# Segment products of an edge block: head outermost instead of sub-block outermost

## What is computed

```python
h = jnp.einsum('nd,hdf->nhf', x, W)                      # 4 heads of 64
a_src = jnp.einsum('nhf,hf->nh', h, att_src)
a_dst = jnp.einsum('nhf,hf->nh', h, att_dst)
e = jax.nn.leaky_relu(a_src[src] + a_dst[dst], NEG_SLOPE)
emax = jax.ops.segment_max(e, dst, num_segments=N)
ex = jnp.exp(e - emax[dst])
denom = jax.ops.segment_sum(ex, dst, num_segments=N)
alpha = ex / denom[dst]
msg = h[src] * alpha[:, :, None]
out = jax.ops.segment_sum(msg, dst, num_segments=N)
```

## Time and profile before

| | us |
|---|---|
| median of 3 runs | 3192.11 |
| lowest and highest | 3185.83, 3193.67 |
| the profiled execution: its time | 3188.82 |
| the same: span from first to last instruction | 3187.0 |
| busy in it: TensorE matmuls / weight loads | 1814.2 / 1333.7 |
| VectorE / ScalarE / GpSimd | 1568.0 / 721.3 / 1911.1 |
| mean granted TensorE clock | 0.641 of full speed |
| first L1136 starts, last L1136 starts | 142.8, 2835.4 |

### The profile page before, as it was taken

One profiled execution on the slowest core, in us unless ns is written; L12 is line 12 of the kernel. 1 busy time (PEld: TensorE's weight loads), 2 busy tenths in 40 slices (PEclk: granted clock), 3 DMA queues, 4 the chain that ended last, 5 costly groups with the idle time before them and its releaser, 6 DMA issues. The chain is left out here.

```text
span 3187.0 us, 54639 instructions
## 1 busy us (share of the span) xinstructions
PE 1814.2 (57%) x17401; PEld 1333.7 (42%) x17401; DVE 1568.0 (49%) x5615; ACT 721.3 (23%) x2125; POOL 1911.1 (60%) x1849
## 2 busy tenths in 40 slices
PE   4666665556665445435435655665566566531995
PEld 3434443444444233223224533553354344321885
DVE  5566665556665454444444445453545444323332
ACT  3522221112222021012003222332232132211221
POOL 1366666666666666666676667666666766731343
PEclk9767765555555555555556666676576667655998
DMA  5244445534444533443355464455545644434787
GB/s 156 89 121 139 140 141 146 159 92 116 129 131 124 136 101 89 108 118 88 89 136 141 124 161 135 120 127 142 137 129 140 168 109 124 129 96 121 199 216 186
DMA packets 275873, 418.72 MB, mean 131 GB/s; under 512 B 70992, under 2 KB 206036, under 8 KB 275336
## 3 DMA queue, kind: packets, MB, share of 16 engines
q0 software_dynamic: 98592, 245.59, 30.3%
q1 hardware_dynamic: 173360, 167.20, 17.3%
q10 hardware_dynamic: 3640, 2.50, 0.3%
HBM read 341.18 MB, written 73.83 MB: 130 GB/s over the span
## 5 line engine op out<-in xcount | busy, mean ns | idle before, releaser
L911 POOL DMA_INDIRECT region<-node_table,region x1612 | 1615.6, 1002 | 979.0 <-issue 442.9
L1136 PE MATMUL ps_p<-region 128*32 128x65 f32 x12896 | 567.5, 290 | 917.4 <-issue 514.4
L1136 PEld LDWEIGHTS ps_p<-region 128*32 128x32 f32 x12896 | 377.8, 147 | 1114.4 <-issue 645.8
L1385 DVE SCALAR_TENSOR_TENSOR acc<-ps_p,region,acc 128x65 f32 x806 | 193.2, 281 | 611.8 <-remote 558.5
L1001 ACT ACTIVATE region<-ps_s 128x128 f32<-128x128 f32 x403 | 111.5, 277 | 1380.9 <-remote 991.4
L1377 DVE TENSOR_TENSOR region<-region 128x512 f32<-128x512 f32 x403 | 280.6, 696 | 147.2 <-DVE region L1361 51.3
L1118 PE MATMUL ps_s<-ident,region 128*128 128x128 f32 x403 | 164.5, 408 | 160.2 <-DVE region L1371 80.0
L1122 PEld LDWEIGHTS ps_s<-region 128*128 128x128 f32 x806 | 204.0, 281 | 94.9 <-issue 64.8
L1007 ACT ACTIVATE region<-region 128x16 f32<-128x16 f32 x403 | 86.9, 216 | 690.3 <-DVE region L1371 348.2
L1357 DVE TENSOR_SCALAR region<-drep,region 128x8 f32 x403 | 101.5, 252 | 258.2 <-issue 257.3
L1122 PE MATMUL ps_s<-region 128*128 128x32 f32 x806 | 191.8, 323 | 24.2 <-issue 23.3
(11 more groups left out here) (317 smaller groups left out, 2807.8 us busy)
## 6 DMA issues: line engine op xcount, KB each, us to landing
region<-in_W_dram SPq DMA_DIRECT2D x84, 512.0 KB
region<-node_table,region POOLq DMA_INDIRECT x1612
acc<-in_W_dram SPq DMA_DIRECT2D x28, 512.0 KB
acc<-base_rows SPq DMA_DIRECT2D x14, 896.0 KB, 5.3
qkv_rows<-region SPq DMA_DIRECT2D x49, 194.0 KB
region<-expert_in SPq DMA_DIRECT2D x28, 258.0 KB
xe<-expert_in SPq DMA_DIRECT2D x28, 258.0 KB, 4.0
node_table<-region SPq DMA_DIRECT2D x49, 132.0 KB, 1.7
```

What stands on the lines that cost most here:

```text
L911: pool.indirect_dma_start(out=rows[:, s, j, :], out_offset=None, in_=table[:, :], in_offset=bass.IndirectOffsetOnAxis(ap=idx[:, s * SUB + ...
L1136: m = pe.matmul(ps_p[s % 2][h * WIN:(h + 1) * WIN, 0:HC], wts[:, s % 2, j, h, :], rows[:, s, j, h * HC:(h + 1) * HC], start=j == 0, stop=j ...
L1385: m = dve.scalar_tensor_tensor(out=a, in0=ps_p[s % 2][:, 0:HC], scalar=here[:, k, at(n)], in1=a, op0=ALU.mult, op1=ALU.add)
```

## The change

The two loops around the matmul are swapped. All sixteen products, their operands, the `start` and `stop` flags and the increment on the last one stay. The last product is (j = 3, h = 3) in both orders.

```diff
@@ -1131,8 +1131,8 @@
                 pe.wait_ge(w_ready, n + 1)
                 if not isinstance(n, int) or n >= 2:
                     pe.wait_ge(block_done, n - 1)
-                for j in range(SUB):
-                    for h in range(G_HEADS):
+                for h in range(G_HEADS):
+                    for j in range(SUB):
                         m = pe.matmul(ps_p[s % 2][h * WIN:(h + 1) * WIN, 0:HC], wts[:, s % 2, j, h, :],
                                       rows[:, s, j, h * HC:(h + 1) * HC], start=j == 0, stop=j == SUB - 1)
                 m.then_inc(block_ps, 1)
```

## The result

| | before | after |
|---|---|---|
| median of 5 runs, us | 3185.83 | 3205.88 |
| lowest and highest | 3180.97, 3193.67 | 3199.32, 3211.06 |
| the profiled execution: time, span | 3188.82, 3187.0 | 3203.76, 3202.0 |
| mean granted TensorE clock | 0.641 | 0.703 |

The ratio of after to before is 1.0062, with a 95% interval of 1.0045 to 1.0079: the new order costs 0.6%, some 20 us. 3228 was forecast, so the sign was right and the size twice too large. Run again on two chips, each time beside the kernel before, the changed kernel came out at 1.0073 (1.0049 to 1.0096) and 1.0060 (1.0046 to 1.0073).

The account below looks back on a forecast made before the run. TensorE completions held while gathers move data were taken as the limit where that cycle runs. Carried blocks' 34 us and projection blocks' 5 us summed to +39 us on the profiled 3188.8, giving 3228 us; range 3100 to 3310.

Parts of the forecast that it names:

- The price of a burst (28 steps): TensorE's sixteen segment products: 28 steps between first and last start, adding 2.26 us at 1.2 GHz, 1.14 at 2.4.
- What of it reaches the end: Whole block loop: of 819 us added on TensorE, 39 us lengthen the run, the rest lies in idle time.
- Light blocks: zero: Blocks without extra TensorE work: ready anew after 4.2 us against a mean period of 6.7 us, so no cost.
- held blocks: hidden: Blocks whose TensorE completions are held during gathers: 12 released records take 1.6 instead of 0.66 us, at no cost.
- 5 stood: The 49 blocks with the projections: 0.1 us each, 5 us.
- the carried blocks' 34 us: Second-half blocks carrying an expert tile, TensorE nearly full: 0.3 us per block, 112 x 0.3 = 34 us.
- the first 244 blocks within 1%: Blocks before the carried expert tiles: the prediction is wrong if their time changes by over 1%.
- Weight loads hidden: Weight loads of the segment products on TensorE: still run beside the matmuls in the new order, adding nothing.
- Rival (d): Segment products: a group's weight load cannot run beside its matmul; about +1.5 us per block, 3790 us; chance 0.07.
- Rival (a), absorbed: Block loop: the holds of completions pace it and the added time sits inside them; 3182 to 3198 us; chance 0.18.
- Rival (b), shorter holds: Held completions in the loop: spreading the burst shortens the holds, -110 us, 3080 us; chance 0.18.
- Rival (c), the clock: TensorE in the loop: being busier, it is granted a higher clock, removing the carried term; 3165 to 3190 us; chance 0.07.

Follow-up runs that it names:

- blocks 0 to 243: The new order in blocks 0 to 243 only, the old order in the rest, against the kernel before: 1.0033 (1.0020 to 1.0046).
- blocks 244 to 402: The new order in blocks 244 to 402 only, the old order in the rest, against the kernel before: 1.0036 (1.0023 to 1.0048).
- blocks 0 to 151: The new order in blocks 0 to 151 only, the old order in the rest, against the kernel before: 1.0022 (1.0008 to 1.0035).
- blocks 152 to 243: The new order in blocks 152 to 243 only, the old order in the rest, against the kernel before: 1.0011 (0.9998 to 1.0024).
- two heads at a time: Kernel before, with the sub-blocks run through for heads 0 and 1 alternating, then 2 and 3: 1.0028 with holds, 0.9994 on the chip of 2825 us.
- three, then the fourth: Kernel before, with each head's sub-blocks 0 to 2 in a row, then the four products of sub-block 3: 1.0081 (1.0055 to 1.0108).
- 164 columns: Kernel before in its old order, each segment product streaming 164 columns instead of 65, VectorE still reading 65: 1.0091 (1.0072 to 1.0109).
- 236 columns: Kernel before in its old order, each segment product streaming 236 columns instead of 65, VectorE still reading 65: 1.0102 (1.0083 to 1.0120).
- the copy taken out: Gathers read row numbers from the resident table without waiting for ScalarE's copy; against the kernel before, old order 0.9978, new order 1.0031.
- the new order and 164 columns: Head order with 164 columns streamed per product instead of 65, against the kernel before on the chip of 2825 us: 1.0102 (1.0082 to 1.0122).

## Why the prediction was right in sign and twice too large

**The price of a burst (28 steps): the step that failed.** Forecast 3.35 and 1.80 us, measured 2.39 and 1.41: +1.30 us at 1.2 GHz and +0.75 at 2.4 instead of +2.26 and +1.14. "The next head's first can start beside the last of the one before" took for granted that records start in program order; the next head starts beside the fourth from the last. At the mean clocks of the earlier trace rows, 19 steps would add 1.23 us per block in the first half and 1.11 in the second, 477 us in all; the higher clock takes some of it back, and measured are 366.8, where the sum had put 819 us.

**What of it reaches the end.** The sum let 39 of 819 us through, 4.8%. Measured against the profiled busy time of L1136 (567.5 before):

| kernel | L1136 busy added, us | slower, us | share | wait for a slot grows by, us |
|---|---|---|---|---|
| the change | 366.8 | 19.7 | 5% | 33 |
| blocks 0 to 243 | 232.2 | 10.5 | 5% | 12 |
| blocks 244 to 402 | 116.8 | 11.5 | 10% | 39 |
| blocks 0 to 151 | 131.4 | 7.0 | 5% | 27 |
| blocks 152 to 243 | 98.4 | 3.5 | 4% | 4 |
| two heads at a time | 126.1 | 8.9 | 7% | 15 |
| three, then the fourth | 203.3 | 25.8 (17.5 to 34.4) | 13% | 34 |
| 164 columns | 429.3 | 29.0 | 7% | 39 |
| 236 columns | 642.4 | 32.5 | 5% | 61 |

All rows are from the chips of 3185 us. The last column is the sum of GpSimd's waits ahead of its gathers for L1136, "remote" and the copy of the row numbers, less the 427 us of before; each is of one profiled execution, and the two other profiles of the changed kernel give 24 and 31.

Four to seven hundredths in most rows, with "blocks 244 to 402" and "three, then the fourth" above them. The interval of the latter begins at 9%, so the share is no constant. For the change itself the share was about right and the price was not: 4.8% of 366.8 is 18 us. This is a regularity of these runs, not a cause.

**Where it lies: wrong.** "Light blocks: zero" and "held blocks: hidden" fail by 0.04 to 0.05 us per block in the first 244, 10.5 us where 5 stood; the carried blocks' 34 us were 11.5 for the whole last part. That the two errors cancel in the share above is luck. The bound that was set, the first 244 blocks within 1%, holds.

**What the light cost is.** The account that the runs fit best: the loop's pace is GpSimd's cycle of gathers, pause and gathers; the pause ends when products of an earlier block are done; and a longer burst moves that by a small part of its length. The waits ahead of L911 grew by 33 us with the change, and with the copy taken out, when the products are all that is waited for, still by 13; they grew in every kernel of the table. What was not isolated is which blocks' products move the pause, and by what part of the added length. Two heads at a time are paid for on a chip that holds (0.28%) and not on the one that doesn't, which points to the pause; but only this order ran on both, and bursts of 3.06 to 5.69 us cost 1.0102 without any hold.

**Weight loads hidden: right.** L1136's weight loads are busy 777.6 us instead of 377.8, since they spread over the burst, and the steps stayed 0.108 us. Rival (d) fell. The rule on loads that the prediction cites with it (the Trainium skill, TensorE: Matmul & The Clock Gate, Part 3, The mechanism) is contradicted here for records of one column group in a row, as it was in the earlier trace rows.

**Rival (a), absorbed** (3182 to 3198): nearly in its mechanism, for about 95% of the added time sits inside waits, but 3205.88 lies above its range. **Rival (b), shorter holds**, fell: 555.4 us of "remote" ahead of L1385 against 558.5. **Rival (c), the clock**: it did rise, 0.641 to 0.703, not over 0.75 in the loop, and took back a part and not all. **The base:** the sum started from the profiled run's 3188.8, and the median before, now of five executions, is 3185.8. That is 3 of the 22 us between 3228 and the 3205.9 measured.

## What to carry to other kernels

Products that write different groups of 32 output partitions ran side by side here, but only as far as the order let them: interleave the groups, or give each at most two fp32 products in a row, which did not lengthen the burst. Price a reordering by its rounds and test that price first in a trace of one burst, then ask separately which share reaches the end; a kernel with the same length in the old order answers that without any argument about the order. Where TensorE had idle time, as here, time added to it came back in part through the clock.

## What was not expected of the hardware

- The starts fit matmul records that overtake those of another group of output partitions: with the change, the ninth record starts beside the fifth, ahead of three others. Five orders of the same 32 records took 7, 19, 11, 7 and 13 steps of 0.108 us.
- The granted clock followed how much TensorE had to do: mean 0.641 for the kernel before, 0.703 with the change, 0.796 with 236 columns, and 0.92 to 0.95 in the loop with the new order and 164 columns.
- The holding of TensorE's completions while gathers run differed by chip: the kernel before takes 3185 us on three chips and 2825 on a fourth, where the three kernels profiled show no such wait.
